# Ternary expert weights made in the context stage and kept in DRAM until the router stage

## What is computed

```python
def _weight_quant(w):
    s = 1.0 / jnp.clip(jnp.mean(jnp.abs(w)), EPS, None)
    return jnp.clip(jnp.round(w * s), -1.0, 1.0) / s
...
logits = jnp.einsum('bsh,eh->bse', x, router_w)
idx = jnp.argmax(logits, axis=-1).reshape(-1)
for e in range(E):
    g = bitlinear(xf, wg[e])
    u = bitlinear(xf, wu[e])
    y = bitlinear(jnp.square(jax.nn.relu(g)) * u, wd[e])
    out = out + jnp.where((idx == e)[:, None], y, 0.0)
```

## Time and profile before

| | us |
|---|---|
| three runs: median (lowest, highest) | 1919.75 (1918.7, 1923.62) |
| profiled execution: its own time / span of the trace | 1915.22 / 1913.5 |
| PE busy | 1493.4 (78%) |
| DVE busy | 1264.8 (66%) |
| ACT busy | 958.2 (50%) |
| POOL busy | 387.4 (20%) |
| mean granted TensorE clock | 0.877 of full speed |
| context / readout / router stage, from the trace | 0 to 236.9 / to 448.7 / to 661.7 |

### The profile page before, as it was taken

The page is one execution under the profiler, slowest core; times in us unless marked ns, Lnnn a source line. Parts: engine busy times, 40 slices in busy tenths (PEclk is TensorE's granted clock), DMA queues, the critical chain, the costliest instruction groups (busy, mean ns, idle before and its releaser), DMA issues. The chain is left out here.

```text
span 1913.5 us, 28222 instructions
## 1 busy us (share of the span) xinstructions
PE 1493.4 (78%) x8535; PEld 826.6 (43%) x8536; DVE 1264.8 (66%) x1600; ACT 958.2 (50%) x1426; POOL 387.4 (20%) x279
## 2 busy tenths in 40 slices
PE   5999889993444277158799999999954669999996
PEld 3444345541444133034144444444422356666663
DVE  4333455553888366663799999999947767655561
ACT  4333234431777156042167676777741367665551
POOL 0000000003000300420155555555665100000000
PEclk8999989996555599568699999999987779999998
DMA  6442300003443122471123342433128467666640
GB/s 236 143 148 110 116 6 0 0 0 133 164 162 132 59 67 88 130 179 60 40 66 95 84 107 73 106 93 87 27 82 236 140 234 261 206 214 228 231 155 32
DMA packets 142468, 226.17 MB, mean 118 GB/s; under 512 B 10424, under 2 KB 60600, under 8 KB 142272
## 3 DMA queue, kind: packets, MB, share of 16 engines
q1 hardware_dynamic: 140352, 219.04, 36.7%
q0 software_dynamic: 2048, 6.33, 1.1%
HBM read 167.65 MB, written 57.49 MB: 118 GB/s over the span
## 5 line engine op out<-in xcount | busy, mean ns | idle before, releaser
L1574 ACT ACTIVATE t_e<-t_psE 128x512 f32<-128x512 f32 x512 | 304.6, 597 | 133.8 <-PE t_psE L1669 113.6
L1613 DVE TENSOR_REDUCE t_nmax<-t_psM 128x1 f32<-128x1024 f32 x256 | 301.5, 1212 | 19.5 <-PE t_psM L1650 19.5
L1532 POOL TENSOR_TENSOR t_low<-t_e 128x1024 bf16<-128x1024 f32 x128 | 249.8, 1953 | 197.9 <-ACT t_e L1574 186.9
L1680 PE MATMUL t_psO<-t_e,vst 128*96 128x512 bf16 x512 | 199.6, 390 | 2.5 <-POOL t_low L1532 2.5
L1669 PE MATMUL t_psE<-t_qst,kst 99*128 99x512 bf16 x512 | 194.9, 382 | 2.6 <-ACT t_e L1574 2.4
L1680 PE MATMUL t_psO<-t_low,vst 128*96 128x512 bf16 x512 | 193.1, 377 | 0.0
L1650 PE MATMUL t_psM<-kst,t_qst 96*128 96x512 bf16 x512 | 164.1, 404 | 31.1 <-DVE t_nmax L1613 22.1
L1621 DVE TENSOR_TENSOR t_low<-t_e 128x1024 bf16<-128x1024 f32 x128 | 173.4, 1355 | 20.5 <-ACT t_e L1574 20.2
L2163 PE MATMUL e_psG<-xeT,e_w1p 128*128 (+1 forms) x1536 | 172.6, 275 | 14.6 <-DVE e_hT L2107 9.9
L2178 PE MATMUL e_psO<-e_w2p,e_hT 128*128 128x512 bf16 x768 | 167.1, 379 | 0.0
L2163 PEld LDWEIGHTS e_psG<-xeT,e_w1p 128*128 128x128 bf16 x1536 | 151.4, 99 | 36.1 <-issue 8.3
(11 more groups left out here) (231 smaller groups left out, 2268.0 us busy)
## 6 DMA issues: line engine op xcount, KB each, us to landing
piece<-in_L_ffn_w SPq DMA_DIRECT2D x32, 1024.0 KB, 14.1
xres<-in_L_ffn_w SPq DMA_DIRECT2D x32, 1024.0 KB, 15.2
values<-c_vst SPq DMA_DIRECT2D x32, 384.0 KB, 2.3
kst<-keys SPq DMA_DIRECT2D x96, 128.0 KB, 4.2
vst<-values SPq DMA_DIRECT2D x16, 768.0 KB, 8.9
mixed<-t_ost SPq DMA_DIRECT2D x64, 192.0 KB
c_rows<-in_ctx SPq DMA_DIRECT2D x8, 1024.0 KB, 6.0
keys<-c_kst SPq DMA_DIRECT2D x32, 256.0 KB, 2.1
```

Source lines behind the costliest of these rows:

```text
L1532: nc.gpsimd.tensor_tensor(low[:, slot(h, u), :, :], e32[:, slot(h, u), :, :], upper(h, u), ALU.subtract).then_inc(lo_pool, 1)
L1574: nc.scalar.activation(e32[:, slot(h, u), i, :], psE[:, i, :], ACT.Exp, scale=SC).then_inc(expd, 1)
L1613: nc.vector.tensor_reduce(nmax[:, h // G % 2, h % G, u:u + 1], banks_of(place_of_max(b, m)).rearrange("p a t -> p (a t)"), AX_X, ALU.max, ...
L1680: last = nc.tensor.matmul(psO[0:VW, h % 2, :], vst[:, g, 2 * u + i, h % G, :], part[:, i, :], start=(u == 0 and i == 0 and r == 0), stop=( ...
```

## The change

All 24 matrices are made ternary in the context stage, in the slots of its gemms, and stored transposed in a DRAM tensor of 12.6 MB (`wt_dram`); the router stage only fetches them into wT. The fp32 matrices (three at a time) and the ternary ones (two) lie in the space of xres, so x is loaded only when they are done, at slots 49 to 54. The first of the three passes (multiply by the reciprocal mean, clip at 1) moves from Vector to GpSimd. For matrix i, `total` on Scalar runs in slot 2i, the mean in slot 2i+2, the pass on GpSimd after it, Vector's two passes in slot 2i+3, and its two halves are transposed, copied and stored in slots 2i+6 and 2i+7 by way of one PSUM bank, psW. All loops over blocks are unrolled. In the router stage the constants that rstd needs come ahead of the clearing memset, Vector waits only for these, the tokens go in groups of four tiles, and the logits stay in PSUM.

```diff
+    AFTER_SUM, AFTER_CLAMP, AFTER_TERN = 2, 3, 6
+    w32 = xres[:, 0:3 * QD, :].rearrange("p (s k) d -> p s k d", k=KC)
+    scratch = ctxT[:, 0:KC, B * T - D:]
+        wout = sb("c_wout", [P, 2, KC, 2 * P], BF16)
+        psW = c.enter_context(nc.psum_tensor("c_psW", [P, 2, KC, P], BF16))
...
+# context, gpsimd
+                for i in range(NW):
+                    pool.wait_ge(rmean_ready, i + 1)
+                    nc.gpsimd.tensor_scalar(w32[:, i % 3, :, :], w32[:, i % 3, :, :], rmean[:, i:i + 1], 1.0,
+                                            ALU.mult, ALU.min).then_inc(scaled, 1)
...
+# context, sync
+                def load_weights(i):
+                    if i >= 3:
+                        sp.wait_ge(cast, i - 2)
+                    sp.dma_start(w32[:, i % 3, :, :], weights[i % 3][i // 3].rearrange("(u p) d -> p u d", p=P)
+                                 ).then_inc(w_loaded[i % 3], 16)
+                def store_weights(h):
+                    i, r = divmod(h, 2)
+                    sp.wait_ge(w_copied, h + 1)
+                    sp.dma_start(wt_dram[i // 3, :, i % 3, :, r * 2 * P:(r + 1) * 2 * P],
+                                 wout[:, r, :, :]).then_inc(w_stored[r], 16)
+                load_ctx(2, 0)
+                for i in range(3):
+                    load_weights(i)
+                load_ctx(3, 1)
+                load_ctx(4, 0)
+                for s in range(8 * NQ):
+                    if s % 8 == 0 and s // 8 + 5 < NQ + 2:
+                        load_ctx(s // 8 + 5, (s // 8 + 5) % 2)
+                    store(s)
+                    if (h := half_at(s)) is not None:
+                        store_weights(h)
+                    if (i := summed_at(s)) is not None and i + 3 < NW:
+                        load_weights(i + 3)
+                    for b in range(B):
+                        if s == 2 * NW + (1, 1, 1, AFTER_TERN)[b]:
+                            load_x(b)
...
+# context, scalar
+                def w_copy(h):
+                    act.wait_ge(w_xposed, h + 1)
+                    if h >= 2:
+                        act.wait_ge(w_stored[h % 2], h // 2 * 16)
+                    nc.scalar.copy(wout[:, h % 2, :, :].rearrange("p k (u s) -> p u k s", s=P), psW[:, :, :, :]).then_inc(w_copied, 1)
+                def total(i):
+                    act.wait_ge(w_loaded[i % 3], i // 3 * 16 + 16)
+                    nc.scalar.activation(scratch, w32[:, i % 3, :, :], ACT.Abs,
+                                         accum_out=absum[:, i:i + 1]).then_inc(abs_done, 1)
+                    for n in range(8):
+                        s = 8 * q + n
+                        evacuate(q, n)
+                        if (h := half_at(s)) is not None:
+                            w_copy(h)
+                        if s % 2 == 0 and s // 2 < NW:
+                            total(s // 2)
...
+# context, vector
+                def ternary(i):
+                    v, m = nc.vector, i % 3
+                    dve.wait_ge(scaled, i + 1)
+                    v.tensor_scalar(w32[:, m, :, :], w32[:, m, :, :], -1.0, MAGIC, ALU.max, ALU.add).then_inc(clamped, 1)
+                    dve.wait_ge(clamped, i + 1)
+                    if i >= 2:
+                        dve.wait_ge(w_xposed, 2 * i - 2)
+                    v.tensor_scalar(tern[:, i % 2, :, :], w32[:, m, :, :], -MAGIC, None, ALU.add).then_inc(cast, 1)
+                    for n in range(8):
+                        evacuate(q, n)
+                        if (i := summed_at(8 * q + n)) is not None:
+                            mean_of(i)
+                        if (i := clamped_at(8 * q + n)) is not None:
+                            ternary(i)
+                        if q == NQ - 1:
+                            statistics(2 * n)
+                            statistics(2 * n + 1)
...
+# context, tensor
+                def w_total(i):
+                    pe.wait_ge(abs_done, i + 1)
+                    if i >= 1:
+                        pe.wait_ge(mean_ready, i)
+                    nc.tensor.matmul(psA[:, i:i + 1], onesf[:, :], absum[:, i:i + 1], start=True, stop=True).then_inc(summed, 1)
+                def w_transposes(h):
+                    i, r = divmod(h, 2)
+                    pe.wait_ge(cast, i + 1)
+                    if h >= 1:
+                        pe.wait_ge(w_copied, h)
+                    for u in range(2):
+                        for k in range(KC):
+                            last = nc.tensor.transpose(psW[:, u, k, :], tern[:, i % 2, 2 * r + u, k * P:(k + 1) * P], ident[:, :])
+                    last.then_inc(w_xposed, 1)
+                    for n in range(8):
+                        s = 8 * q + n
+                        if (i := summed_at(s)) is not None:
+                            w_total(i)
+                        if (h := half_at(s)) is not None:
+                            w_transposes(h)
+                        gemm(q, n)
...
+# router, gpsimd
+                done(nc.gpsimd.memset(rows[:, :], 0.0))
+                done(nc.gpsimd.memset(half[:, :], -0.5))
+                done(nc.gpsimd.tensor_scalar(veps[:, :], moments[:, :, 1], EPS, None, ALU.add))
+                done(nc.gpsimd.tensor_tensor(rstd[:, :], veps[:, :], half[:, :], ALU.pow))
                 nc.gpsimd.memset(wT[:, E - 2:E, :, :, :], 0.0).then_inc(zero_set, 1)
                 pool.wait_ge(zero_set, 1)
...
+# router, sync
+                for e in range(E):
+                    if e == E - 2:
+                        sp.wait_ge(zero_stored, 16)
+                    fetch(e)
...
+# router, scalar
+                for t in range(NT):
+                    x_copy(t)
+                    if t + QD < NT:
+                        high(t + QD)
+                    integers(t)
...
+# router, vector
+                dve.wait_ge(consts, RSTD)
+                for t in range(QD):
+                    normalise(t)
+                for g in range(B):
+                    if g + 1 < B:
+                        for t in range((g + 1) * QD, (g + 2) * QD):
+                            normalise(t)
+                    scale(g)
+                    for t in range(g * QD, (g + 1) * QD):
+                        low(t)
+                        quantise(t)
...
+# router, tensor
+                for t in range(NT):
+                    if t + 1 < NT:
+                        x_transposes(t + 1)
+                    judge(t)
```

More of the change, by code:

```diff
@@ L106, in _ @@
                                  g.rearrange("(o n) -> o n", o=1).to_broadcast([P, 2])).then_inc(gates_loaded, 16)
[L107 to L120, removed]
+                load_ctx(2, 0)
[14 more added lines that the diff above has]
+                            load_x(b)
+                for r in range(2):
+                    sp.wait_ge(w_stored[r], 16 * NW)
                 for k in range(2):
@@ L154, in evacuate @@
                                              bias=bias[:, k:k + 1]).then_inc(hi_out, 1)
-                    for k in range(QD):
-                        act.wait_ge(gemm_done, q * 8 + k + 5)
+                    else:
                         act.wait_ge(v_stored[k % 2], q * 32 + k // 2 * 16 + 16)
@@ new lines, in gemm @@
+                def gemm(q, n):
+                    if n == 0:
+                        pe.wait_ge(even_copied, 2 * q + 7)
+                        pe.wait_ge(odd_copied, 2 * q + 7)
+                    pe.wait_ge(lo_out, q * 8 + n + 1)
+                    k = n % QD
+                    for i, (a, b) in enumerate((x + c, y + c) for x, y in ((0, 0), (0, KC), (KC, 0)) for c in range(KC)):
+                        if n < QD:
+                            last = nc.tensor.matmul(psG[:, k, :], wT[:, 0, a, k * P:(k + 1) * P],
+                                                    ctxT[:, b, q * 512:(q + 1) * 512], start=(i == 0), stop=(i == 11))
+                        else:
+                            last = nc.tensor.matmul(psG[:, k, :], ctxT[:, a, q * 512 + k * P:q * 512 + (k + 1) * P],
+                                                    wT[:, 1, b, :], start=(i == 0), stop=(i == 11))
+                    last.then_inc(gemm_done, 1)
@@ L695, in x_copy @@
-                def x_copy(t, j):
-                    act.wait_ge(xposed, t + 3)
-                    act.wait_ge(judged, t + 1)
-                    nc.scalar.copy(xT[:, j, :, :], psX[:, :, :]).then_inc(xcopied, 1)
-                def w_copy(e, m, n):
-                    act.wait_ge(w_xposed, n + 4)
-                    for i in range(2):
-                        last = nc.scalar.copy(wT[:, bass.ds(e, 1), m, :, i * 2 * P:(i * 2 + 2) * P].rearrange(
-                            "p o k (u s) -> p (o u) k s", s=P), psW[:, i, :, :, :])
-                    last.then_inc(w_copied, 1)
@@ L723, in _, with high, integers @@
-                for s, n in ((q_cast, 2), (xcopied, 1), (w_copied, 1)):
-                    act.sem_inc(s, n)
-                act.wait_ge(consts, 1)
+                def high(t):
```

(8 more changed lines are left out.)

372 lines of the change are left out of this document (145 added, 227 removed).

## The result

Median **1971.07 us** (1969.66 to 1973.02, 4 runs) against 1921.68 (1918.70 to 1924.03) for the kernel before on the same chip: ratio 1.0259, 95% interval 1.0238 to 1.0279. Forecast were 1940 us and a range of 1900 to 1985. The sign was right; of the profiled executions' difference of 57 us (1915.2 to 1972.3) the forecast had 20.

The account below looks back on a forecast made before the run. Vector was taken to bound the router stage, Tensor the context stage. Context terms 112 + 2 + 15 + 6 + 5 = +140 us, router -120, net +20: 1935 profiled, forecast 1940 us, range 1900 to 1985.

Parts of the forecast that it names:

- Copy loop: Context stage: Tensor's transposes wait for Scalar's evacuation and copy, 4.92 us a slot against 2.59, 48 slots, +112 us.
- Start: Context stage: three weight loads go in front of the fourth block of context, +6 us (0 to 8).
- Clock: Context stage: slow matmuls after stretches of waiting at six block boundaries and some late-store slots, +5 us (0 to 20).
- a low clock (2010): Rival, context stage: clock falls to 1.2 GHz in half of the 48 slots, +72, 2010 us; chance 0.11.
- the DMA queue as the bound (1965): Rival, context stage: small pieces at half rate, 11 us a pair with waits, +25, 1965 us; chance 0.11.
- Stores behind the load: Context stage, SyncE queue: the odd half's store lands 1.7 us late behind a 1 MB load, +15 us (0 to 30).
- GpSimd's pass: Context stage: pass over 128x2048 fp32 takes 2.5 us, hidden under a cover of 4.5 us; even 4.8 costs almost nothing.
- 9 us or more: Rival, context stage: GpSimd's pass far slower than the rows, +4 us a pair, about 2030 us; chance 0.04.
- Router stage, -120: Router stage: first logits reduction at 509.6 us instead of 628.97, Vector starting after GpSimd's memset; gain 120 us (112 to 130).
- the variant of 124: Router stage: Vector's first normalisations slip in before the memset under the lock rule, a gain of 124 us instead.
- The weight fetch is hidden: Router stage: fetch of ternary weights ends near 505 us, scatter near 542; 37 us of cover, else 40 us.
- The rival that the copy wait hides: Context stage: Scalar copies before its slot's matmuls end, 1836 us; faster below 1.9 us added per slot; chance 0.09.

Follow-up runs that it names:

- edits 2 and 3: Changed kernel with GpSimd's first pass moved to Vector and the weight load issued one slot later, behind the odd slot's stores: 1921.71 us, ratio 1.0032.
- all three edits: Changed kernel with Scalar copying before it evacuates, the first pass on Vector, and the weight load behind the odd slot's stores: 1888.97 us, ratio 0.9845.
- with the load between: Changed kernel with the first pass on Vector and the weight load issued between the key or value store and the half's store: 1939.00 us, ratio 1.0096.
- the kernel with one operation: Changed kernel with GpSimd's pass cut to the product, without the clip: pass 5.44 us instead of 7.16, context stage ends at 398.6 us instead of 420.9.
- The last kernel: Changed kernel with copy first, pass on Vector, load later, four half buffers, and the weight slots' memset on Vector: 1868.07 us, ratio 0.9735.
- edit 1: Changed kernel with Scalar's copy of a weight half put ahead of the evacuation of the same slot: 1980.45 us, ratio 1.0316.

## Why the prediction was right in sign and wrong in size

The stages' differences account for all of it: +184.0 - 3.1 - 124.4 = +56.5 of 57.1 us.

- **Copy loop, 112 us: right.** 4.97 us a slot instead of 4.92. The kernel with edits 2 and 3 is the one that the forecast's loop describes: context stage 369.6, by the terms 236.9 + 5.2 (start) + 48 x 2.38 + 2 = 358.3, and 3.9 for the clock (next point but one) are 362.2. The other 7.4 us, some one a block, I have not traced.
- **Start, 6 us: right.** The first group starts at 39.40 instead of 34.24.
- **Clock, 5 us: right for that kernel.** In it seven groups took 3.24 to 4.85 us instead of 2.75, 9.4 us together. The kernel before already had 5.5 of such (four runs of 48 matmuls took 11.27 to 12.22 us instead of 10.52), so 3.9 are added. In the changed kernel they come to some 20 us; the surplus is a consequence of its late slots and lies inside the next two terms. The rivals of a low clock (2010) and of the DMA queue as the bound (1965) didn't happen: the granted clock is 0.89 and the DMA share 0.55, and the kernel with all three edits moves the same bytes in a context stage of 334.7 us. That 1965 lies nearest to the measured time is luck. (My sizes there were off: a half is 256 KB, so 0.52 MB a pair and not 1.05.)
- **Stores behind the load, 15 us: this is the step that failed.** The prediction named both stores, "the odd slot's key or value store and the store of its weight half", and then followed the half's alone. The other, unpriced, costs 25.0: its buffer is wanted two slots on by Scalar's *evacuation*, which stands ahead of the cast that releases the next load, so its lateness is part of the loop that issues the next load, twice in a block. That the half's 15 us meet 14.4 measured is luck: they were reckoned with a half of 0.52 MB, and with its true 0.26 the lateness shrinks from 1.7 us to about 0.8, less than the 1.0 that the prediction lets be absorbed, so its own reckoning would give next to nothing. In the changed kernel the copy waits only 0.9 us for its stores; the 14.4 show once the evacuations no longer wait (16.3 us with the load between).
- **GpSimd's pass, 2.5 us at no cost: wrong.** It took 7.16, outside the bounds of 1.7 to 4.8 taken from the nearest rows, a memset and a two-input pass with one operation. The cover of 4.5 us was reasoned within one pair and not from one pass to the next. The loop from pass to pass is 7.16 + 3.5 us, since Vector's next mean is queued behind the passes that wait for this one. That alone costs 28.0 (397.6 against 369.6), and 11.9 on top of the late stores (420.9 against 409.0; 22.3 by the kernel with one operation, whose loop of 5.44 + 3.5 us no longer binds). The rival "9 us or more" had the right mechanism and too high a threshold.
- **The sum**: 132.7 (all that the kernel with edits 2 and 3 has) + 14.4 + 25.0 + 11.9 = 184.0. The split of the last 51.3 us hangs on the order in which the causes are added: stores first it is 39.4 and then 11.9 for GpSimd's pass, GpSimd first it is 28.0 and then 23.3 for the stores. The prediction had 15 for both.
- **Router stage, -120: right, and the measured 124.4 is not the variant of 124.** The memset blocked Vector as the forecast had it: the first four normalisations took 12.12 us instead of the 1.91 of the next four, and Scalar's first copy of a tile came 24.5 us into the stage (forecast 25.2). Nothing slipped in ahead of the memset; that the numbers agree is luck. What was mis-sized is Scalar's part: its 16 tiles took 30.3 us and not 35.2, since the high halves of the first four tiles are made before its loop and a tile takes 1.94 us and not 2.2. The first reduction came 55.5 us into the stage (forecast 60.9), the rest took 33.1 (32.8). The Trainium skill (SBUF — State Buffer, the section on the two separate sides) has this as an exclusive lock that goes to the instruction which starts first, for its whole length, while the other blocks fully. This trace agrees on the full block. On who gets it the rows do not: the memset's row starts 0.02 us after Vector's and it ran its usual 10.34 us. Whether a row's start is the moment at which the lock is taken, no run shows. The last kernel took the memset off GpSimd and gained 7.9 us.
- **The weight fetch is hidden, as forecast**: issued at 644.55 to 654.6, landing a median 23.7 us after issue; the DMA engines' busy share is 0.99 or more from 676 to 682 us and 0.34 from 682 to 684, so it ends near 683, while the first reduction is at 685.08 and the mixture's first load at 718.17.

The rival that the copy wait hides, with its break-even, was the way out: edit 1 opens it, yet only once the other two loops are gone (34.9 us then, -4.3 before).

## What to carry to other kernels

For each wait that a change adds, write down the closed loop that runs through it: what must have happened an iteration before, on which queue, behind what. The period is at least the longest loop, and two loops through the same engines can add up in part (here 13.7 us a pair from loops of 10.7 and 10.6, with the clock's falls in it). Edits to a shorter loop can be worth nothing, or less, until the longer is gone, so an edit that gains nothing alone is not refuted. When a large load waits on a semaphore in an in-order queue, put every small store whose buffer is wanted soon ahead of it. And for an operation that no row shows, bound the loop that it sits in, and say at what duration it begins to bind (here 6.4 us: 9.94 less 3.5).

## What the runs showed of the hardware that I had not expected

- GpSimd needs 3.5 ns an element a partition for a two-operation tensor_scalar over fp32 (7.16 us for 128x2048), 2.7 ns for one operation, where Vector needs 0.60 to 0.63 (1.23 to 1.28 us); a memset of bf16 there is 0.84 ns.
- Stores of 256 KB that land in 2.1 us in the kernel before take a median 6.4 in the changed one, where one in two is issued right behind a load of 1 MB in the same queue that itself takes 6.2. The key store of 102.52 us, issued 0.41 us behind its load, freed its buffer 6.4 us later. With the order changed, the one that goes ahead of the load takes 2.8 and the one behind it 6.1.
- Tensor's first group of 12 matmuls behind a wait of 5.2 to 5.5 us (110.78, 166.13, 220.54 and 330.20 us in the changed kernel) took 4.72 to 5.20 us instead of 2.75, and the next was back at 2.75; behind waits of 1.6 to 1.8 us it stayed at 2.75. Such a wait costs 2.0 to 2.5 us of clock on top of itself.
- A normalisation on Vector whose row starts 0.02 us before that of a GpSimd memset of 10.34 us took 10.64 us instead of 0.54.
